# GNN layer and mixture of experts on one core: GpSimd's block loop written out with fixed index columns, two of six gathers moved ahead of the join, the row normalisation on ScalarE moved ahead of the masked copies

## The chip, the cores and the metric

The kernel runs on one core of a Trainium2 chip. The metric is the device time of one execution, in microseconds (us). TensorE (PE in the rows) does the matmuls, VectorE (DVE), ScalarE (ACT) and GpSimd (POOL) the element work, SyncE (SP) only issues transfers. GpSimd also issues every indirect transfer (a gather or a scatter by a column of row numbers).

## The reference

There are 6250 nodes of 256 features and 100000 edges of 96 features, sorted by their target node `dst`. A GNN layer, then a mixture of 16 experts, both with a residual:

```python
xn = layernorm(x)
out1 = segment_sum(edge_attr, dst);  cnt = segment_sum(1, dst)
out2 = where(cnt > 0, segment_max(edge_attr, dst), 0)
out3 = out1 / max(cnt, 1)
h = concat([xn, out1, out2, out3, u[0]])
x = x + (relu(h @ W1 + b1) @ W2 + b2 + xn)
y = layernorm(x);  two best experts of y @ gate_w + gate_b, softmax of the two
moe = weighted sum of the two expert MLPs (256 -> 512 -> 256)
x = x + layernorm(y + moe) * gamma + beta
```

## The kernel before

**Stages.** From 0 to about 117 us indices are made, from there to about 765 us the GNN layer runs, then 113 expert tiles until about 1210 us, then the last sums and norms. The prediction is about the GNN layer.

**Edges.** The edges are cut into ten chunks of 128 pieces of 80 edges. VectorE scans one chunk after another (`edges`), running sums and running maxima from the end of the edge list to its start, and SyncE stores the results to DRAM (`run_sum`, `run_max`, `piece_carry`), raises `chunk_done` when a chunk has landed and then loads the edges of a later one.

**Nodes.** The 6250 nodes are worked off in 25 blocks (`MACROS`) of two tiles (index `a`) of 125 rows, highest nodes first. For block i+1, while TensorE works on block i:

- GpSimd gathers, per tile, the rows of `run_max` (into `GM`), `run_sum` (`GS`) and `piece_carry` (`GC`) at which the nodes begin: six indirect transfers (lines 639 to 641), issued two blocks ahead. The row numbers stand in `IX`, two columns a tile. `gatei` holds, per block, how many chunks must be in DRAM (its level, 1 to 10); GpSimd loads it into a register (line 629), and one of ten branches (line 636) holds the six gathers with that many chunks as the transfers' source.
- `cut` (GpSimd, 646) and `carry_in` (ScalarE, 874 to 882) work out what a node takes from the next piece; `join` (GpSimd, 650 to 654) adds it up into `RAW`; `mask_rows` (ScalarE) makes six masked copies into `NB` (906 to 908), and then the two normalised tiles `XN` (912).
- TensorE's `turn` (1155, 1158) transposes `XN` and `NB`; it waits for `node_rows`, raised by the last operation of `mask_rows`.

**TensorE's step** for block i is: first half of layer 1 (1174, 1176, 1178), router of block i-2 (1207), second half of layer 1, `turn` of block i+1, layer 2 (1188) with `turn_x2` of block i-1 (1200) in its middle. The second half of layer 1 waits for the first half's relu, which ScalarE does (926) behind `carry_in` of block i+1.

**GpSimd's step** (`rows_step`) for block i is: `add_rows` (668; waits until ScalarE has taken layer 2 of block i-1 out, 976), `residual` (685, 687), `cut`, `norm1` (659 to 663) and `join` of block i+1, `norm2` (673 to 678) of block i-1, `gather` of block i+2. Steps 2 to 21 are in a hardware loop of two steps a turn (`in_pairs`); since the block number is then in a register, `gather` first copies the four index columns to `IXn` (631), and waits for that copy.

All engines run in the order in which their code is written, and wait on semaphores alone.

Of the kernel before, what the change touches and what calls it, by code (L numbers as in the profile page):

```python
# [98 lines left out]
def after(i, g, b, n=1):  # L99

    return i + n, g + (b + n) // 2, (b + n) % 2


def gnn_moe_kernel(nc, x, dst, edge_attr, u, gW1, gb1, gW2, gb2, gate_w, gate_b,
# [47 lines left out]
    ALONE = (SURE - 7) // 4 * 4  # L152
    KEYS = 8192
# [40 lines left out]
    with ExitStack() as ctx:  # L194
# [75 lines left out]
        IXn = [a.take(2, 2, parts=NT, dt=U32) for _ in range(2)]  # L270
# [117 lines left out]
        ix_copied, carried, joined, node_rows = sem("ix_copied"), sem("carried"), sem("joined"), sem("node_rows")  # L388
# [191 lines left out]
        def _(pool):  # L580
# [47 lines left out]
            def gather(i, g, b):  # L628
                level = pool.value_load(gatei[0:1, bass.ds(MACROS - 1 - i, 1)], min_val=1, max_val=LEVELS)
                hold(pool, turned, i + 1)  # L630
                pool.tensor_copy(IXn[b], IX[:, bass.ds(2 * (MACROS - 1 - i), 2), :]).then_inc(ix_copied, 1)
                pool.wait_ge(ix_copied, i + 1)
                hold(pool, chunk_done, level * LEVEL)
                for lv in range(1, LEVELS + 1):
                    edges, pieces = lv * LEVEL * P * T, lv * LEVEL * P
                    with pool.If(level == lv):
                        for a in range(2):
                            last, before = (bass.IndirectOffsetOnAxis(IXn[b][:, a, n:n + 1], 0) for n in range(2))
                            pool.indirect_dma_start(out=GM[b][:, a, :], out_offset=None, in_=s_max[0:edges], in_offset=last).then_inc(gathered[b], 16)  # L639
                            pool.indirect_dma_start(out=GS[b][:, a, :], out_offset=None, in_=s_sum[0:edges], in_offset=last).then_inc(gathered[b], 16)  # L640
                            pool.indirect_dma_start(out=GC[b][:, a, :], out_offset=None, in_=carry[0:pieces], in_offset=before).then_inc(gathered[b], 16)
# [47 lines left out]
            def rows_step(i, g, b):  # L689
                more = not isinstance(i, int) or i + 1 < MACROS  # L690
                norm = not isinstance(i, int) or i >= 1
                if norm:
                    add_rows(i - 1)
                residual(i, g, b)
                if more:
                    cut(*after(i, g, b))
                    norm1(i + 1)
                    join(*after(i, g, b))
                if norm:
                    norm2(i - 1)  # L700
                if not isinstance(i, int) or i + 2 < MACROS:
                    gather(*after(i, g, b, 2))
            pool.sem_inc(joined, 1)
            gather(0, 0, 0)
# [3 lines left out]
            gather(1, 0, 1)  # L708
            rows_step(0, 0, 0)
            rows_step(1, 0, 1)  # L710
            pool.wait_ge(index_ready, 2)
            in_pairs(pool, MACROS, rows_step, ahead=3, first=2)
# [96 lines left out]
        def _(act):  # L809
# [91 lines left out]

            def mask_rows(i, g, b):
                act.wait_ge(joined, i + 2)
                for a in range(2):
# [3 lines left out]
                    act.activation(NB[b][:, a, 2 * P:3 * P].rearrange("p (n r) -> p n r", n=QUAD), spread(RAW[b][:, a, 0, EF - REST:EF], 1, QUAD),  # L908
                                   ACT.Identity, scale=rch[:, j])
                act.wait_ge(rstd1_ready, i + 1)  # L910
                for a in range(2):
                    ins = act.activation(XN[b][:, a, :], XR[b][0:NT, a, :], ACT.Identity, bias=nmr_1[:, a:a + 1], scale=rstd_1[:, a:a + 1])  # L912
# [66 lines left out]
            def gnn_step(i, g, b, to=None):  # L979
# [19 lines left out]
                if more:  # L999
                    mask_rows(*after(i, g, b))  # L1000
# [859 lines left out]
```

## Time and profile before

| | us |
|---|---|
| median of 3 runs (1270.43 to 1273.61) | 1272.97 |
| the profiled execution | 1271.26 |
| its span, first to last instruction | 1269.4 |
| PE busy | 1097.0 (86%) |
| POOL busy | 807.2 (64%) |
| DVE busy | 832.5 (66%) |
| ACT busy | 647.6 (51%) |

The page and the views of the trace count time in us from the span's start. "busy" leaves out what an engine's queue does for itself (register work, branches, waits, the issuing of plain transfers); such records stand under POOLq, ACTq or SPq. A bracket at a row's end says how long the engine stood idle ahead of that row, and what ended it.

### The profile page before, as it was taken

The numbers are of one execution on the slowest core, as the hardware profiler recorded it, in microseconds if no ns is written. First come the engines' busy times: TensorE is split into PE (matmuls) and PEld (weight loads), VectorE is DVE, ScalarE is ACT, GpSimd is POOL, SyncE is SP. The second block draws the span as 40 slices with busy tenths as digits, with TensorE's granted clock in tenths as the row PEclk, the third lists the DMA queues.
The fourth block names the chain that finished last, engine by engine and source line by source line (L and its number), as shares of the span: only waits on it lengthen the run. The fifth ranks groups of instructions, "written<-read, shape, count | busy, mean of one in ns | idle before, by whom it ended". The sixth has DMA issues, their size and how long they took to land.

```text
span 1269.4 us, 27454 instructions
## 1 busy us (share of the span) xinstructions
PE 1097.0 (86%) x6460; PEld 955.6 (75%) x6461; DVE 832.5 (66%) x3164; ACT 647.6 (51%) x1974; POOL 807.2 (64%) x1056
## 2 busy tenths in 40 slices
PE   2002999999999999999999999889999999999935
PEld 1002888888888888887888788789999999999911
DVE  4989999899989989980367811366322222247788
ACT  5863565566556656665566534222323232345554
POOL 4886657666666666666676525556666566657586
PEclk7555999999999999998999999899999999999975
DMA  9995768777776785479111146776666676688855
GB/s 318 282 306 181 256 232 311 253 271 286 268 259 249 293 259 204 169 286 315 54 38 47 30 154 203 261 250 200 204 209 213 205 217 214 208 295 293 282 178 155
DMA packets 131327, 282.70 MB, mean 223 GB/s; under 512 B 25900, under 2 KB 38576, under 8 KB 131114
## 3 DMA queue, kind: packets, MB, share of 16 engines
q1 hardware_dynamic: 94230, 218.41, 50.2%
q0 software_dynamic: 26048, 43.47, 11.3%
q10 hardware_dynamic: 10964, 19.96, 4.6%
q14 instruction: 64, 0.52, 0.1%
q8 instruction: 21, 0.34, 0.1%
HBM read 167.27 MB, written 114.25 MB: 222 GB/s over the span
## 4 chain that ended last, share of the span: by engine, by line
PE 57%; POOL 11%; issue 10%; DMA 8%; ACT 7%; DVE 3%; POOLq 2%; ACTq 1%; SPq 0%; DVEq 0%
PE ps L1299 16%; PE ps L1307 15%; PE ps L1188 7%; PE ps L1174 7%; PE ps L1176 6%; DMA mem<-piece_carry,mem 4%; DMA mem<-in_dst_dram,mem 2%; POOL mem L639 2%; POOL mem L640 2%; POOL mem L622 2%; PE ps L1285 2%; ACT mem L926 1%; POOL mem L791 1%; PE ps L1178 1%; POOL mem L797 1%
## 5 line engine op out<-in xcount | busy, mean ns | idle before, releaser
L1026 ACT ACTIVATE mem<-ps,mem 128x128 f32<-128x128 f32 x452 | 129.3, 368 | 284.6 <-PE ps L1299 283.8
L1299 PEld LDWEIGHTS ps<-mem 128*128 128x128 f32 x1808 | 220.6, 194 | 18.9 <-issue 12.2
L1299 PE MATMUL ps<-mem 128*128 128x128 f32 x1808 | 224.8, 278 | 10.2 <-issue 9.6
L1174 PE MATMUL ps<-mem 128*128 128x250 f32 x800 | 209.3, 384 | 11.7 <-ACT mem L926 10.0
L1307 PE MATMUL ps<-mem 128*128 x904 | 214.8, 381 | 0.7 <-issue 0.7
L1396 DVE TENSOR_TENSOR_SCAN mem<-ps,mem 128x80 f32<-128x80 f32 x960 | 208.0, 304 | 0.3
L1400 DVE TENSOR_TENSOR_SCAN mem<-ps,mem 128x80 f32<-128x80 f32 x960 | 207.9, 308 | 0.0
L1176 PE MATMUL ps<-mem 128*128 128x250 f32 x800 | 205.0, 379 | 0.0
L1188 PE MATMUL ps<-mem 128*125 128x256 f32 x800 | 182.4, 381 | 0.7 <-ACT mem L926 0.7
L1307 PEld LDWEIGHTS ps<-mem 128*128 128x128 f32 x904 | 163.8, 191 | 18.8 <-issue 0.9
L1174 PEld LDWEIGHTS ps<-mem 128*128 128x128 f32 x800 | 153.3, 194 | 31.6 <-ACT mem L926 12.3
L1176 PEld LDWEIGHTS ps<-mem 128*128 128x128 f32 x800 | 154.1, 193 | 18.8
L1188 PEld LDWEIGHTS ps<-mem 128*125 128x125 f32 x800 | 147.3, 189 | 21.5 <-ACT mem L926 1.1
L1679 DVE TENSOR_TENSOR mem<-ps,mem 128x256 f32<-128x256 f32 x113 | 48.0, 425 | 150.9 <-PE ps L1307 115.6
L734 POOL DMA_INDIRECT expert_rows<-mem x90 | 91.6, 1018 | 85.6 <-DVE mem L1679 66.1
L1672 DVE COPY mem<-ps 128x256 f32<-128x256 f32 x113 | 47.8, 423 | 136.4 <-PE ps L1285 132.8
L727 POOL DMA_INDIRECT mem<-x_normed,mem x96 | 96.1, 1001 | 34.0 <-issue 16.8
L926 ACT ACTIVATE mem<-ps,mem 128x250 f32<-128x250 f32 x200 | 77.1, 468 | 46.5 <-PE ps L1178 46.5
L1155 PE MATMUL ps<-mem 125*128 125x125 f32 x100 | 20.6, 288 | 90.8 <-ACT mem L912 90.8
L639 POOL DMA_INDIRECT mem<-run_max,mem x50 | 63.8, 1277 | 46.4 <-issue 46.1
L1155 PEld LDWEIGHTS ps<-mem 125*128 125x128 f32 x100 | 11.5, 144 | 97.9 <-issue 97.9
L622 POOL DMA_INDIRECT mem<-in_dst_dram,mem x50 | 62.8, 1255 | 27.2 <-issue 12.5
(284 smaller groups left out, 1677.2 us busy)
## 6 DMA issues: line engine op xcount, KB each, us to landing
mem<-in_L_ffn_w_dram SPq DMA_DIRECT2D x129, 512.0 KB, 9.4
run_sum<-mem SPq DMA_DIRECT2D x80, 480.0 KB
run_max<-mem SPq DMA_DIRECT2D x80, 480.0 KB
mem<-in_edge_attr_dram SPq DMA_DIRECT2D x72, 480.0 KB, 8.2
mem<-expert_rows SPq DMA_DIRECT2D x26, 256.0 KB, 5.5
x_rows<-mem ACTq DMA_DIRECT2D x25, 256.0 KB, 4.4
x_normed<-mem ACTq DMA_DIRECT2D x25, 256.0 KB
mem<-in_x_dram ACTq DMA_DIRECT2D x24, 256.0 KB
```

The lines of the kernel that those rows point to most:

```text
L639: pool.indirect_dma_start(out=GM[b][:, a, :], out_offset=None, in_=s_max[0:edges], in_offset=last).then_inc(gathered[b], 16)
L727: pool.indirect_dma_start(out=XG[q], out_offset=None, in_=x2_d[0:rows], in_offset=bass.IndirectOffsetOnAxis(slot_now[q % 2], 0)).then_inc( ...
L734: pool.indirect_dma_start(out=ya_d, out_offset=bass.IndirectOffsetOnAxis(into_now[b], 0), in_=YO[b], in_offset=None).then_inc(yo_stored[b] ...
L926: act.activation(H[:, hc, :], bank(H_BANKS[q][hc - q * QUAD], 0, M), ACT.Relu, bias=cbias[:, hc:hc + 1]).then_inc(h_ready, 1)
L1026: ins = act.activation(hT[b][:, c, :], bank(2 + b, c * P, (c + 1) * P), ACT.Relu, bias=eb1c[:, bass.ds(e, 1), c])
L1174: pe.matmul(h, W1x[:, c, hc * P:(hc + 1) * P], XT[b][:, c, :], start=(c == 0), stop=False)
L1176: pe.matmul(h, W1a[:, s, hc * P:(hc + 1) * P], AT[b][:, s, :], start=False, stop=False)
L1188: ins = pe.matmul(bank(5, a * D, (a + 1) * D, NT), H[:, hc, a * NT:(a + 1) * NT], W2[:, hc, :], start=(hc == 0), stop=(hc == HC - 1))
L1299: ins = pe.matmul(bank(2 + b, f * P, (f + 1) * P), w1now[q][:, c, f * P:(f + 1) * P], XgT[b][:, c, :], start=(c == 0), stop=(c == DC - 1))
L1307: ins = pe.matmul(bank(6 + b, 0, D), hT[b][:, c, :], w(c * D, D), start=(c == 0), stop=(c == FC - 1))
L1396: ins = dve.tensor_tensor_scan(out=Sb[:, ::-1, f], data0=keep[b][:, ::-1], data1=Eb[b][:, ::-1, f], initial=0.0, op0=ALU.mult, op1=ALU.add)
L1400: ins = dve.tensor_tensor_scan(out=Eb[b][:, ::-1, f], data0=bound[b][:, ::-1], data1=Eb[b][:, ::-1, f], initial=-FMAX, op0=ALU.min, op1=AL ...
```

## The change

- GpSimd's step is written out 25 times with the block number as a constant. The six gathers read their columns of `IX` in place; the copy to `IXn`, the wait for it and the wait for `turned` are gone.
- The ten branches become at most two. `SCANNED` holds, per block, a number of chunks `near`; a block of a level up to `near` waits for `near` chunks and gathers from them, one of a higher level waits for all ten. Where `near` is ten there is no branch and no load. For the input of the reference the levels of blocks 0 to 24 are 1, 1, 1, 1, 2, 2, 2, 2, 2, 3, 3, 3, 3, 4, 4, 4, 5, 5, 5, 6, 6, 7, 7, 8, 10, and `near` is 1, 1, 1, 1, 2, 2, 3, 3, 3, 4, 4, 5, 5, 6, 6, 7, 7, 8, 8, 9, 9, 9, 10, 10, 10, so that the second branch is never taken.
- Of the six gathers of block i+2 the first `AMID` = 2 (`GM` and `GS` of tile 0) are issued behind `norm1` and ahead of `join` of block i+1, the other four behind `norm2` of block i-1. They were all six behind `norm2`.
- On ScalarE the two `XN` operations stand ahead of the six masked copies, as `norm_rows`.

```diff
+    SCANNED = [1 if i < 4 else min(LEVELS, 1 + (24 * (i - 2) + 10) // 52) for i in range(MACROS)]
+    AMID = 2
...
-            def gather(i, g, b):
-                level = pool.value_load(gatei[0:1, bass.ds(MACROS - 1 - i, 1)], min_val=1, max_val=LEVELS)
-                hold(pool, turned, i + 1)
-                pool.tensor_copy(IXn[b], IX[:, bass.ds(2 * (MACROS - 1 - i), 2), :]).then_inc(ix_copied, 1)
-                pool.wait_ge(ix_copied, i + 1)
-                hold(pool, chunk_done, level * LEVEL)
-                for lv in range(1, LEVELS + 1):
-                    edges, pieces = lv * LEVEL * P * T, lv * LEVEL * P
-                    with pool.If(level == lv):
...
+            def by_level(i, body):
+                near = SCANNED[i]
+                if near == LEVELS:
+                    body(LEVELS)
+                else:
+                    level = pool.value_load(gatei[0:1, MACROS - 1 - i:MACROS - i], min_val=1, max_val=LEVELS)
+                    with pool.If(level < near + 1):
+                        body(near)
+                    with pool.If(level > near):
+                        body(LEVELS)
...
+                def behind_cut(levels):
+                    if levels:
+                        pool.wait_ge(chunk_done, levels * LEVEL)
+                        gather_rows(i + 2, 0, AMID, levels)
+                    if i + 1 < MACROS:
+                        join(*after(i, g, b))
+                    if i:
+                        norm2(i - 1)
+                    if levels:
+                        gather_rows(i + 2, AMID, 6, levels)
...
+            for i in range(MACROS):
+                rows_step(i)
...
+            def norm_rows(i, g, b):
+                act.wait_ge(rstd1_ready, i + 1)
+                for a in range(2):
+                    act.activation(XN[b][:, a, :], XR[b][0:NT, a, :], ACT.Identity, bias=nmr_1[:, a:a + 1], scale=rstd_1[:, a:a + 1])
...
                 if more:
+                    norm_rows(*after(i, g, b))
                     mask_rows(*after(i, g, b))
```

GpSimd's queue in one step of the block loop, before, from `join` on (`mem` is the core's SBUF; ISA and branch rows are the queue's own work):

```order
L650 TENSOR_TENSOR mem<-mem 125x2x96 [waits carried]
L651 TENSOR_TENSOR mem<-mem 125x192
L652 TENSOR_TENSOR mem<-mem 125x192
L654 TENSOR_TENSOR mem<-mem 125x2x96 [waits picked]
L673 TENSOR_SCALAR mem<-mem 125x2 [waits moments2_step]
L676 TENSOR_TENSOR mem<-mem 125x2 [waits norm2_step]
L678 TENSOR_TENSOR mem<-mem 125x2 [waits norm2_step]
L629 TENSOR_LOAD mem
L629 ISA x2
L631 COPY mem<-mem 125x4 [waits turned]
L636 COMPARE_AND_BRANCH [waits ix_copied,chunk_in_dram]
L639 DMA mem<-run_max,mem 125x96
```

The same place now, from the last operation of `norm1` (L676 in the new numbering) on:

```order
L644 TENSOR_LOAD mem
L644 ISA x2
L645 COMPARE_AND_BRANCH
L636 DMA mem<-run_max,mem 125x96 [waits chunk_in_dram]
L636 DMA mem<-run_sum,mem 125x96
L663 TENSOR_TENSOR mem<-mem 125x2x96 [waits carried]
L664 TENSOR_TENSOR mem<-mem 125x192
L665 TENSOR_TENSOR mem<-mem 125x192
L667 TENSOR_TENSOR mem<-mem 125x2x96 [waits picked]
L686 TENSOR_SCALAR mem<-mem 125x2 [waits moments2_step]
L689 TENSOR_TENSOR mem<-mem 125x2 [waits norm2_step]
L691 TENSOR_TENSOR mem<-mem 125x2 [waits norm2_step]
```

The load of the level, the branch and two gathers now stand ahead of the join (L663 to L667), and four gathers follow the last row; the copy is gone.

ScalarE's queue ahead of the first `turn`, before, behind the last operation of `carry_in`:

```order
L906 ACTIVATE mem<-mem 125x192 [waits joined]
L907 ACTIVATE mem<-mem 125x64
L908 ACTIVATE mem<-mem 125x128
L906 ACTIVATE mem<-mem 125x192
L907 ACTIVATE mem<-mem 125x64
L908 ACTIVATE mem<-mem 125x128
L912 ACTIVATE mem<-mem 125x256 [waits norm1_rstd_ready]
L912 ACTIVATE mem<-mem 125x256
```

And now:

```order
L929 ACTIVATE mem<-mem 125x256 [waits norm1_rstd_ready]
L929 ACTIVATE mem<-mem 125x256
L935 ACTIVATE mem<-mem 125x192 [waits joined]
L936 ACTIVATE mem<-mem 125x64
L937 ACTIVATE mem<-mem 125x128
L935 ACTIVATE mem<-mem 125x192
L936 ACTIVATE mem<-mem 125x64
L937 ACTIVATE mem<-mem 125x128
```

The two 125x256 operations now stand ahead of the wait for `joined`, and the masked copies are the last thing ahead of `node_rows`.

## Rows read from the trace of the kernel before

**Rows 1.** Waits of PE, 95 to 765 us: total us, times, longest us
```profile
PE ps L1155 <- ACT mem L912: 90.8, 1, 90.8
PE ps L1174 <- ACT mem L926: 10.0, 13, 2.5
```
**Rows 2.** Timeline of PE, block starts and one `turn`: start us, us, operation
```profile
172.19 1.01 PE L1174 MATMUL ps<-mem 128*128 128x250 f32 x4
...
375.62 1.01 PE L1174 MATMUL ps<-mem 128*128 128x250 f32 x4
...
391.58 0.43 PE L1155 MATMUL ps<-mem 125*128 125x125 f32 x2
...
400.04 1.01 PE L1174 MATMUL ps<-mem 128*128 128x250 f32 x4
...
628.39 1.01 PE L1174 MATMUL ps<-mem 128*128 128x250 f32 x4
```
**Rows 3.** Timeline of PE in block 7
```profile
306.30 1.11 PE L1174 MATMUL ps<-mem 128*128 128x250 f32 x4 [1.36 <-ACT mem L926]
307.25 1.62 PE L1176 MATMUL ps<-mem 128*128 128x250 f32 x4
```
**Rows 4.** Timeline of POOL in block 10 and the start of block 11
```profile
382.63 0.20 POOL L663 TENSOR_TENSOR mem<-mem 125x2 f32<-125x2 f32 x1
383.59 0.59 POOL L650 TENSOR_TENSOR mem<-mem 125x192 f32<-125x192 f32 x1 [0.76 <-ACT mem L882]
...
385.38 0.60 POOL L654 TENSOR_TENSOR mem<-mem 125x192 f32<-125x192 f32 x1
...
388.99 0.20 POOL L678 TENSOR_TENSOR mem<-mem 125x2 f32 x1 [0.27 <-POOL mem L676]
...
391.65 1.33 POOL L639 DMA_INDIRECT mem<-run_max,mem  x1 [1.43 <-issue]
393.28 1.21 POOL L640 DMA_INDIRECT mem<-run_sum,mem  x1 [0.30 <-issue]
...
399.35 1.21 POOL L641 DMA_INDIRECT mem<-piece_carry,mem  x1 [0.30 <-issue]
401.18 1.43 POOL L668 TENSOR_TENSOR mem<-mem 125x512 f32<-125x512 f32 x1 [0.62 <-ACT mem L976]
```
**Rows 5.** Chain that ended last, block 2, then block 10: start us, us, what
```profile
186.01 1.24 POOLq L629
...
389.13 0.29 POOLq L629
...
390.73 0.92 issue
...
399.35 6.83 DMA mem<-piece_carry,mem
```
**Rows 6.** Waits of POOL, 100 to 765 us: the gaps ahead of the copy
```profile
POOL mem L631 <- issue: 25.1, 24, 2.0
```
**Rows 7.** Timeline of ACT in block 10: first masked copy, the two normalisations
```profile
388.16 0.45 ACT L906 ACTIVATE mem<-mem 125x192 f32<-125x192 f32 x1 [0.92 <-ACT mem L940]
...
389.93 1.08 ACT L912 ACTIVATE mem<-mem 125x256 f32<-125x256 f32 x2
```
**Rows 8.** Timeline of POOL, ACT and PE at the start of the layer
```profile
95.28 0.20 POOL L631 COPY mem<-mem 125x4 uint32<-125x4 uint32 x1
96.52 1.22 POOL L639 DMA_INDIRECT mem<-run_max,mem  x1 [1.04 <-issue]
...
116.35 1.08 ACT L912 ACTIVATE mem<-mem 125x256 f32<-125x256 f32 x2
...
117.69 0.65 PE L1155 MATMUL ps<-mem 125*128 125x125 f32 x2 [90.75 <-ACT mem L912]
```
**Rows 9.** Timeline of SP: edge loads, issued when the third chunk is done
```profile
198.04 4.42 SPq L440 DMA_DIRECT2D mem<-in_edge_attr_dram  x8
```
**Rows 10.** Timeline of PE in block 22: the expert tables' matmul
```profile
706.85 0.76 PE L1224 MATMUL ps<-mem 125*128 125x172 bf16 x4 [2.30 <-DVEq L1522]
```

More of the change, by code:

```diff
@@ new lines, in gather_rows @@
+            def gather_rows(i, lo, hi, levels):
+                b = i % 2
+                edges, pieces = levels * LEVEL * P * T, levels * LEVEL * P
+                for n in range(lo, hi):
+                    j, a = 2 * (MACROS - 1 - i) + n // 3, n // 3
+                    into, rows = ((GM[b], s_max[0:edges]), (GS[b], s_sum[0:edges]), (GC[b], carry[0:pieces]))[n % 3]
+                    kind = 1 if n % 3 == 2 else 0
+                    pool.indirect_dma_start(out=into[:, a, :], out_offset=None, in_=rows,
+                                            in_offset=bass.IndirectOffsetOnAxis(IX[:, j, kind:kind + 1], 0)).then_inc(gathered[b], 16)
@@ new lines, in by_level, with gather, all_rows @@
+            def by_level(i, body):
[8 more added lines that the diff above has]
+                        body(LEVELS)
+            def gather(i):
+                def all_rows(levels):
+                    pool.wait_ge(chunk_done, levels * LEVEL)
+                    gather_rows(i, 0, 6, levels)
+                by_level(i, all_rows)
@@ L687, in residual, with rows_step @@
                 pool.tensor_tensor(RES, RES, b2bc, ALU.add).then_inc(residual_ready, 1)
[L689 to L692, printed above, removed]
+            def rows_step(i):
+                g, b = i // 2, i % 2
+                def behind_cut(levels):
+                    if levels:
+                        pool.wait_ge(chunk_done, levels * LEVEL)
+                        gather_rows(i + 2, 0, AMID, levels)
[5 more added lines that the diff above has]
+                        gather_rows(i + 2, AMID, 6, levels)
+                if i:
                     add_rows(i - 1)
                 residual(i, g, b)
-                if more:
+                if i + 1 < MACROS:
                     cut(*after(i, g, b))
                     norm1(i + 1)
[L698 to L702, printed above, removed]
+                if i + 2 == (TILES - LATE) // 2:
+                    pool.wait_ge(index_ready, 2)
+                if i + 2 < MACROS:
+                    by_level(i + 2, behind_cut)
+                else:
+                    behind_cut(0)
             pool.sem_inc(joined, 1)
-            gather(0, 0, 0)
+            gather(0)
             norm1(0)
@@ L707, in _ @@
             join(0, 0, 0)
[L708 to L712, printed above, removed]
+            gather(1)
+            for i in range(MACROS):
+                rows_step(i)
             def next_from(i, h, q):
@@ L907, in mask_rows @@
                     act.activation(NB[b][:, a, 2 * EF:2 * P], RAW[b][:, a, 0, 0:EF - REST], ACT.Identity, scale=rch[:, j])
[L908 to L912, printed above, removed]
+                    ins = act.activation(NB[b][:, a, 2 * P:3 * P].rearrange("p (n r) -> p n r", n=QUAD), spread(RAW[b][:, a, 0, EF - REST:EF], 1, QUAD),
+                                         ACT.Identity, scale=rch[:, j])
                 ins.then_inc(node_rows, 1)
```

9 lines of the change are left out of this document (2 added, 7 removed).

## The prediction

> **What bounds the kernel now.** I read the page's table of slices first: PE is at eight tenths or more from the fifth slice on to the last two, so any gain must come from the start, from PE's few waits, or from the last stage, which the change doesn't touch. The waits of PE in the GNN stage [rows 1] are two things: 90.8 us until the first `turn`, ended by the last normalisation on ACT, and 13 waits of 10.0 us in all for the first relu. The block starts [rows 2] give the size of the second: blocks 2 to 19, 18 of them, take 628.39 - 172.19 = 456.20 us. Block 10 takes 400.04 - 375.62 = 24.42 with PE never idle, and 18 of these are 439.56. So 16.6 us are lost, more than the 10.0 of waits, because a long wait is followed by slow matmuls: behind 1.36 us idle in block 7 four matmuls take 1.62 us and not 1.01 [rows 3].
>
> The relu is late because ACT stands in `carry_in`, waiting for the last gather. In block 10 that gather is issued at 399.35 and lands 6.83 us later, at 406.18, which is 6.14 into block 11 [rows 4, 5]; there it costs 0.48 us, and block 11 is one of the mild ones. POOL can't issue it sooner: its six gathers begin 2.66 us behind the start of the last `norm2` operation (391.65 - 388.99) and are 1.5 us apart [rows 4]. **So POOL's chain of one step sets the loss, at the landing of the sixth gather.**
>
> **The start (-1.9 us).** Ahead of the first gather the copy goes: it starts at 95.28 and the gather at 96.52, 1.24 us later; a gap of 0.30 as between two gathers is left, which saves 0.94 [rows 8, 4]. `norm1` of block 0 is long done when ACT reaches the masked copies (ACT then waits for the join), so the two normalisations, 116.35 to 117.43, leave the path: 1.0 us saved. Together 1.9, all on the path, as PE waits for nothing else there.
>
> **POOL's step.** In block 10 `norm1`'s last operation starts at 382.63. Behind it now come the load, the branch and two gathers. The load of the level ended 0.43 behind the start of the operation ahead of it (389.13 + 0.29 against 388.99); between the last branch and the first gather lie 0.92 us [rows 4, 5]. Register work between load and branch isn't separable from the copy's in these rows; it lies between 0.1 and 1.3 us (the branch at 390.73 follows the load's end by 1.31 with the copy in between), and I take 0.4, nearer the low end, since the copy, its semaphore and one or two branches go. So the first gather starts 0.43 + 0.4 + 0.92 = 1.75 us behind, at 384.38, the second 1.63 later at 386.01, and the join at 387.25. The join lasts 2.39 (383.59 to 385.98), to 389.64. It ended at 385.98 before: **3.7 us later**, of which the 0.76 wait for `carry_in` in front of it was free anyway.
>
> Who waits for that is ACT, with the masked copies, then relu and the taking out of `turn`, queued behind. ACT reaches them at 388.16 [rows 7]; now it first does the normalisations there, to about 389.2, and then waits for the join. From 389.70 the six copies last 1.85 (388.16 to 389.93, and a tail of 0.1), and PE sees them 0.26 later (117.69 against 117.43 [rows 8]), at 391.81. PE gets to `turn` at 391.58 [rows 2]. **So each block may wait about 0.25 us at `turn`, a wait that wasn't there.** Without the edit on ACT it would be 1.1 more. The bounds: with the first gather starting as soon as a gather follows another (0.30 for 0.92) there is none; with the whole 2.66 us of rows 4 kept, 0.9 more, 1.15.
>
> Some loads of the level are long: 1.24 us at 186.01 against 0.29 at 389.13 [rows 5]. The gaps ahead of the copy sum to 25.1 us in 24 [rows 6]; at 0.87, a quick one's length, they would be 20.9, so the long loads cost 4.2, or 0.18 a step. They were absorbed in POOL's step; now they stand ahead of the join and reach PE: 18 x 0.18 = 3.3 us.
>
> The Trainium skill, Runtime: NRT & Kernel Launch, Instruction fetch mechanics, has a register load at about 200 ns each, a round trip. The quick loads of this trace are near it (0.29), the long ones aren't; by the page's figure, an estimate, these 3.3 us would be nought. The trace decides, and I keep them.
>
> What it buys: `norm2` now follows the join, and its three operations end at about 391.4, and four gathers follow, the last starting at about 396.9 instead of 399.35, 2.5 us earlier. With the same 6.83 it lands at 403.7, 3.7 into block 11, ahead of `cut` (405.3) and `carry_in`. POOL is free at about 398.1, 2.9 us ahead of `add_rows` (401.18), where it had 0.6 [rows 4]. So the waits at the relu should go, all 16.6 us, slow matmuls with them.
>
> **Free edits.** Waiting for `near` chunks and not for the level: the tightest case is the third chunk, done at 198.04 [rows 9] and first asked for in block 4 at about 229; nothing waits. The branches to 2 from 10, the `turned` wait and the loop's own branches go without a price; they lay in the gap of 2.66 or beside gathers.
>
> **Blocks 20 to 24.** PE waits there for VectorE's tables (2.30 us at 706.85 [rows 10]), which start from the router's logits of an earlier block; they move with the earlier blocks, and nothing further is gained or lost.
>
> **The sum**, against the profiled execution's 1271.26 (span 1269.4): start -1.9; blocks 0 and 1 at 0.25 each, +0.5; blocks 2 to 19: 18 x (24.42 + 0.25) + 3.3 = 447.4 for 456.2, -8.8. Together -10.2, or 1261.1. The median of the runs is 1.7 above the profiled one; against it the forecast is 1272.97 - 10.2 = **1262.8 us**.
>
> **Rivals.** (B) The join is never late: the 0.92 us in front of the first gather runs while `norm1` does, and long loads hide in the same place. For it: between two gathers only 0.30 is seen. Against: the gap was there at 390.73 with nothing else to do. It gives the start and all of 16.6: 1272.97 - 18.5 = 1254.5.
>
> (C) **Slower: the join is late and takes the place of the relu.** Its place is `turn`; its price the upper bound, 1.15 + 0.18 = 1.33 us in each of 20 blocks, 26.6, against 18.5 gained: 1281. Waits of that length were followed by slow matmuls [rows 3], which would add to it. It decides from a mean lateness of 18.5 / 20 = 0.93 us. Against it: my 0.25 would have to be out by 0.7, and POOL's step starts no later than in block 10, since `add_rows` now has slack.
>
> (D) The landing doesn't follow the issue: the four last gathers meet the stores of the scanned chunks, and land as late as ever, or the small waits at `turn` and at a few relus add up to what the relu's did. Then the start alone is left: about 1271. Against: 2.5 us earlier is a third of the 6.83.
>
> (E) The unrolled code stalls at its branches. The rows have ten branches a step, and a jump back every second step, without a gap of a transfer's length in them. If each skipped body cost a wait like one landing (6.83) less the 2.9 of slack, 20 x 3.9 less 18.5 would give 1332. The Trainium skill, same page and section, says that a taken branch whose target isn't in the current window makes the queue fetch it by DMA before going on; it also says that this favours full unrolling. By that rule this rival's place is behind the sixth gather, where two branches are taken.
>
> **How the numbers follow.** Forecast 0.52 (alone 1258 to 1268, the 0.25 and the 0.18 being free within about 0.3 a block), B 0.20, C 0.10, D 0.16, E 0.02. A measurement of this kernel tells about 0.3%, 3.8 us, from no change. Faster by more holds the forecast, B and a sliver (0.02) of D, 0.74; the same is the rest of D, 0.14; slower C and E, 0.12. The range 1254 to 1272 leaves out C, E, a part of D and the low end of B.
>
> **What would show it.** The first `turn` at about 115.8 us instead of 117.69. PE's waits for ACT's relu near nought, and in their place waits at `turn`, some 20 of about 0.25 and three to five of 1 us, behind long loads. On POOL 1.75 us from `norm1`'s last operation to the first gather. No row of POOL waiting for SP's chunks. Block starts 24.5 to 24.8 apart. The prediction is wrong if blocks 2 to 19 take under 442 or over 452 us, or if the part behind block 19 changes by more than 2.

## The result and the profile after

The changed kernel takes 1253.32 us (median of 4 runs, 1251.29 to 1254.82), where the kernel before takes 1272.97. The ratio is 0.985, with a 95% interval of 0.982 to 0.987: 19.6 us less, nearly twice the 10.2 that I forecast, and 0.7 us outside my range. The profiled execution is 1254.82 us long, with a span of 1252.9, against 1271.26 and 1269.4 before. So the two traces, on which all that follows rests, explain 16.4 us; the other 3.2 are how each profiled execution stands to its own median (1.7 below it before, 1.5 above it after). In the later runs a few executions are more than 1.5% longer than the fastest of their kernel, and the ratios leave those out.

First the waits of PE, 95 to 765 us, of the kernel after (total us, times, longest us), which answer to [rows 1]. `turn` is now line 1183, layer 1 is 1202, the masked copies end on 937 and the relu is 952.

```profile
PE ps L1183 <- ACT mem L937: 89.7, 7, 87.7
...
PE ps L1202 <- ACT mem L952: 1.7, 3, 0.7
```

The waits for the relu were 10.0 us in 13 and are 1.7 in 3. The waits at `turn` are 7, one of which is the first block's 87.7, so 2.0 us are left for the other six. Now PE's timeline, with the first `turn` of the layer, the starts of blocks 0, 2, 10, 11 and 20, the longest of the six waits and the `turn` of block 10; it answers to [rows 2, 8].

```profile
115.64 0.65 PE L1183 MATMUL ps<-mem 125*128 125x125 f32 x2 [87.73 <-ACT mem L937]
...
119.38 1.20 PE L1202 MATMUL ps<-mem 128*128 128x250 f32 x2 [1.43 <-ACT mem L945]
...
170.11 1.01 PE L1202 MATMUL ps<-mem 128*128 128x250 f32 x4
...
366.68 1.01 PE L1202 MATMUL ps<-mem 128*128 128x250 f32 x4
...
382.64 0.43 PE L1183 MATMUL ps<-mem 125*128 125x125 f32 x2
...
391.10 1.01 PE L1202 MATMUL ps<-mem 128*128 128x250 f32 x4
...
603.70 0.43 PE L1183 MATMUL ps<-mem 125*128 125x125 f32 x2 [0.52 <-ACT mem L937]
...
612.17 1.01 PE L1202 MATMUL ps<-mem 128*128 128x250 f32 x4
```

The first `turn` came at 117.69 and comes at 115.64: 2.05 us at the start, in this pair of executions (more on that at e1). Blocks 2 to 19 take 612.17 - 170.11 = 442.06 us and took 456.20: 14.14. Blocks 0 and 1 take what they took (50.73 for 50.76), and so do blocks 20 to 23; 0.3 us less lie behind them. That is the whole 16.4, within a tenth. The floor of 18 x 24.42 = 439.56 is nearly reached, and block 10, at 391.10 - 366.68 = 24.42, has no wait at `turn`.

POOL in block 10, which answers to [rows 4]:

```profile
373.44 0.19 POOL L676 TENSOR_TENSOR mem<-mem 125x2 f32<-125x2 f32 x1
374.87 1.32 POOL L636 DMA_INDIRECT mem<-run_max,mem  x1 [1.24 <-issue]
376.50 1.21 POOL L636 DMA_INDIRECT mem<-run_sum,mem  x1 [0.31 <-issue]
377.74 0.60 POOL L663 TENSOR_TENSOR mem<-mem 125x192 f32<-125x192 f32 x1
...
379.52 0.60 POOL L667 TENSOR_TENSOR mem<-mem 125x192 f32<-125x192 f32 x1
...
386.94 1.21 POOL L636 DMA_INDIRECT mem<-piece_carry,mem  x1 [0.30 <-issue]
392.14 1.28 POOL L681 TENSOR_TENSOR mem<-mem 125x512 f32<-125x512 f32 x1 [3.99 <-ACT mem L1002]
```

The sixth gather starts 20.3 us into the block, and started at 23.7; `add_rows` (line 681) finds POOL idle for 3.99 us where it was 0.62. The join, 377.74 to 380.12, ends 13.4 us into the block, where it ended at 10.4. From here on a time "into the block" counts from the first layer-1 matmul of that block.

What stands between `norm1`'s last operation and the first gather is to be seen in the chain that ended last, a step with a short load (block 10) and one with a long load (block 16): start us, us, what.

```profile
373.40 0.23 POOLq L644
373.63 0.10 issue
373.73 0.16 POOLq L644
...
373.97 0.04 POOLq L645
374.01 0.86 issue
374.87 1.32 POOL mem L636
...
520.21 0.23 POOLq L644
520.44 0.81 issue
521.25 0.15 POOLq L644
...
521.47 0.04 POOLq L645
521.51 0.86 issue
```

The load of the level (line 644) shows in the chain as 0.23 us and then as an "issue" of 0.10 us in one case and 0.81 in the other, which is the rest of the same load: it lasts 0.3 us in the first case and 1.0 in the second. The branch (645) costs 0.04 and is followed by 0.86 us in both. These are the two parts of my 1.75 us, and I come back to them.

### The profile page after: what moved, and what is told of

It is laid out like the page before. It is cut to its first block, busy times and chain, and to the rows that moved or that the text cites. A ratio compares the mean times of both kernels' runs of the same rounds, so it can differ in the third digit from the quotient of the medians.

```text
span 1252.9 us, 26862 instructions
## 1 busy us (share of the span) xinstructions
PE 1088.9 (87%) x6460; PEld 949.9 (76%) x6461; DVE 838.2 (67%) x3164; ACT 650.1 (52%) x1974; POOL 804.0 (64%) x1030
## 4 chain that ended last, share of the span: by engine, by line
PE 40%; POOL 29%; issue 17%; DVE 4%; ACT 4%; DMA 4%; POOLq 1%; SPq 0%; DVEq 0%; ACTq 0%
PE ps L1327 16%; PE ps L1335 15%; POOL mem L636 12%; DMA mem<-in_dst_dram,mem 2%; POOL mem L698 2%; POOL mem L681 2%; POOL mem L700 2%; PE ps L1216 2%; PE ps L1313 2%; PE ps L1202 2%; PE ps L1204 2%; ACT mem L852 2%; POOL mem L623 1%; POOL mem L689 1%; POOL mem L674 1%
## 5 line engine op out<-in xcount | busy, mean ns | idle before, releaser
L1327 PE MATMUL ps<-mem 128*128 128x128 f32 x1808 | 223.8, 278 | 10.9 <-issue 10.4
L1202 PE MATMUL ps<-mem 128*128 128x250 f32 x800 | 205.4, 379 | 3.1 <-ACT mem L952 1.7
L1204 PE MATMUL ps<-mem 128*128 128x250 f32 x800 | 202.2, 375 | 0.0
L681 POOL TENSOR_TENSOR mem<-mem 125x512 f32<-125x512 f32 x25 | 32.6, 1303 | 118.2 <-ACT mem L1002 118.2
```

The costliest lines, as they stand in the source:

```text
L1202: pe.matmul(h, W1x[:, c, hc * P:(hc + 1) * P], XT[b][:, c, :], start=(c == 0), stop=False)
L1204: pe.matmul(h, W1a[:, s, hc * P:(hc + 1) * P], AT[b][:, s, :], start=False, stop=False)
L1327: ins = pe.matmul(bank(2 + b, f * P, (f + 1) * P), w1now[q][:, c, f * P:(f + 1) * P], XgT[b][:, c, :], start=(c == 0), stop=(c == DC - 1))
```

## The experiments

All are compared with the kernel before on their own chip, whose median was 1275.22 us for the first four, 1272.06 for the next four and 1278.06 for the last four. Three stretches that hardly depend on the edits differ by some us from execution to execution: what lies ahead of block 2 (it starts at 170.1 to 173.5 us, in e8 at 177.2), block 22 (29.8 to 33.3 us long) and what lies behind the start of block 24, the expert stage above all (527 to 536 us). The kernel after alone has 170.1 and 173.2 for the first and 31.7 and 33.3 for the second in its two profiled executions. So the totals scatter, and the sharper number of each trace is the length of blocks 2 to 19, the stretch in which the change acts. All of it in one table (the last two columns are the lowest and the highest of blocks 2 to 18, in us into the block, from POOL's timeline). The first column is the median of all executions; the ratio is worked out from the single executions and differs from that of the two medians by up to 0.003:

```
                                         us  ratio [95%]             blocks 2-19                join ends   6th gather
before                              1272.97                       628.39-172.19=456.20  10.3-13.0   23.7-26.9
after                               1253.32  0.985 [0.982,0.987]  612.17-170.11=442.06  13.4-14.5   20.2-21.5
e1_after_again                      1256.96  0.983 [0.979,0.988]  615.20-173.22=441.98  13.3-14.5   20.2-21.3
e2_norms_behind                     1272.4   0.997 [0.996,0.999]  628.33-173.12=455.21  13.4-14.4   20.2-21.2
e3_none_ahead                       1251.82  0.980 [0.976,0.984]  609.83-170.39=439.44  10.2-10.7   21.5-21.7
e4_one_ahead                        1251.92  0.980 [0.976,0.985]  611.47-172.02=439.45  11.8-12.8   20.2-21.2
e5_norms_only                       1281.74  (see there)          632.53-170.82=461.71  10.2-14.2   23.7-28.6
e6_none_ahead_norms_behind          1248.63  0.981 [0.977,0.985]  609.73-170.28=439.45  10.2-10.7   21.5-21.6
e7_load_early                       1252.13  0.983 [0.979,0.987]  610.55-171.11=439.44  12.8-13.2   19.6-20.0
e8_three_ahead                      1288.13  1.011 [1.007,1.015]  646.53-177.19=469.34  14.9-15.9   20.2-21.8
e9_unrolled_only                    1269.5   0.995 [0.992,0.997]  624.35-173.49=450.86  10.1-12.5   22.8-26.6
e10_ten_branches                    1257.08  0.984 [0.982,0.986]  611.49-170.94=440.55  10.1-10.9   22.4-23.9
e11_copy_back                       1259.34  0.985 [0.982,0.988]  611.11-171.73=439.38  10.2-10.7   21.5-21.9
e12_two_copies                      1256.0   0.982 [0.979,0.985]  612.89-173.51=439.38  10.2-10.7   21.6-22.0
```

**The change once more.** The kernel after without an edit.

> The changed kernel as it is, timed again beside the kernel before and the three variants of this series. The two profiled executions differ by 16.4 us and the medians by 19.6. If the profiled execution of the changed kernel was a long one of its own spread, the new ratio lies at 0.985 to 0.987 and blocks 2 to 19 again take about 442 us; if the difference of the medians is real beyond the trace, a part outside blocks 2 to 19 must be shorter in this trace.

It was 1256.96 us, a ratio of 0.983, with 442.0 us for blocks 2 to 19: the gain and its place are both there again. The start isn't. The first `turn` comes 1.53 us later than in the first execution of the same kernel, and block 2 starts at 173.22, 1.0 us later than in the kernel before:

```profile
117.17 0.65 PE L1183 MATMUL ps<-mem 125*128 125x125 f32 x2 [88.53 <-ACT mem L937]
```

**ScalarE's edit undone.** The kernel after, with

```
-    norm_rows(*after(i, g, b))
     mask_rows(*after(i, g, b))
+    norm_rows(*after(i, g, b))
```

> ScalarE's edit undone: the two normalisations behind the masked copies again, all else as changed. Theory (the join now ends at 13.4 us of a block and turn is due at 15.96): copies and normalisations need 2.85 us behind the join and 0.26 to reach TensorE, so turn waits 0.65 us in a plain block and 0.6 more behind a long load: 20 x 0.65 + 4, and 1.0 at the start, about 16 us more than the changed kernel, 1269. Rival (the edit is worth only its 1.0 us at the start): 1254.5.

It was 1272.4 us, 15.4 more than e1 where I expected about 16, and the join's end stayed where the kernel after has it. PE in block 10 of this kernel, and ScalarE ahead of that (the masked copies are lines 936 to 938 here, the normalisations 929):

```profile
391.52 0.43 PE L1183 MATMUL ps<-mem 125*128 125x125 f32 x2 [1.08 <-ACT mem L929]
```
```profile
388.62 0.46 ACT L936 ACTIVATE mem<-mem 125x192 f32<-125x192 f32 x1 [2.66 <-POOL mem L667]
...
390.09 0.39 ACT L938 ACTIVATE mem<-mem 125x128 f32<-125x128 f32 x1
390.38 1.08 ACT L929 ACTIVATE mem<-mem 125x256 f32<-125x256 f32 x2
```

ScalarE had stood idle for 2.66 us until the join was done, copied, and then normalised, and PE waited 1.08 us for it at `turn`. So in the kernel after ScalarE's edit carries nearly the whole gain (13.2 us in blocks 2 to 19). The next runs say that the edit by itself isn't worth 13 us.

**No gather ahead of the join, and one.** The kernel after with

```
-    AMID = 2
+    AMID = 0
```

and, for the other, `AMID = 1`.

> AMID = 0: all six gathers behind norm2, with fixed columns and two branches. Theory (the gain is the dropped copy, its wait and the branches, since the sixth gather then starts at 22.5 us of a block and lands at 4.9 of the next, just ahead of cut at 5.0): 1253 to 1257, with waits at the relu of 0 to 3 us in all and none at turn. Rival (the two gathers ahead of the join are what frees the chain): most of the old waits stay, 1262 to 1270.

> AMID = 1: one gather ahead of the join. Theory: the join ends at 11.9 us of a block instead of 13.4, norm2 still ends at 13.5 because it waits for ScalarE, and the sixth gather starts at 20.4 as against 20.2; so the 2.0 us of waits at turn go and nothing is lost: 1251 to 1252. Rival (each gather ahead of the join buys 1.5 us of landing that some blocks need): up to 1256.

Neither was slower than the kernel after; in the stretch both are 2.6 us shorter, with no wait at `turn` behind the first block's. PE's waits of e3, 95 to 765 us, and then POOL in its block 10, whose start is at 365.69:

```profile
PE ps L1183 <- ACT mem L937: 87.6, 1, 87.6
```
```profile
375.43 0.60 POOL L667 TENSOR_TENSOR mem<-mem 125x192 f32<-125x192 f32 x1
377.45 0.19 POOL L686 TENSOR_SCALAR mem<-mem 125x2 f32<-125x2 f32 x1 [1.42 <-ACT mem L966]
...
378.69 0.20 POOL L691 TENSOR_TENSOR mem<-mem 125x2 f32<-125x2 f32 x1 [0.18 <-POOL mem L689]
379.50 1.33 POOL L636 DMA_INDIRECT mem<-run_max,mem  x1 [0.61 <-issue]
...
387.21 1.21 POOL L636 DMA_INDIRECT mem<-piece_carry,mem  x1 [0.31 <-issue]
```

All six gathers come behind `norm2`, and still the sixth starts 21.5 us into the block and not 23.7. From the start of `norm2`'s last operation to the first gather it is 0.81 us, where [rows 4] had 2.66. So the rival of e3, that the two early gathers free the chain, is out. The two gathers that the change put ahead of the join buy only the last 1.2 us, and nothing waits for these.

**ScalarE's edit alone, on the kernel before.** The normalisations go ahead of the masked copies, and nothing on POOL changes:

```
-                act.wait_ge(rstd1_ready, i + 1)
-                for a in range(2):
-                    ins = act.activation(XN[b][:, a, :], ...
...
+                norm_rows(*after(i, g, b))
                 mask_rows(*after(i, g, b))
```

> The kernel before with ScalarE's edit alone (normalisations in front of the masked copies); GpSimd's loop, copy, level branches and gathers as they were. Theory (ScalarE's edit is worth something only at the start and where GpSimd's join is late; in the kernel before the join ends at T+10.4 and the normalisations end ahead of the turn at T+15.96): only the 1.0 us at the start, 1272 where before is 1273, ratio 0.999, blocks 2 to 19 still near 456 us. Rival (the normalisations on the way to the turn cost every block by themselves): about 0.8 us in each of 20 blocks, 1257, ratio 0.987.

It gained nothing: blocks 2 to 19 took 461.7 us in the profiled execution of 1273.12 us. Its four executions took 1270.85, 1273.12, 1290.37 and 1293.12 us, too far apart for a ratio; the two short ones lie on either side of 1272.06, the median of the kernel before. The waits for the relu (line 928 here) were 15.4 us in 10, as they were 10.0 in [rows 1]:

```profile
PE ps L1178 <- ACT mem L928: 15.4, 10, 3.7
```

The rival (12 us or more gained) is out. The theory's 456 was 5.7 too low; what the late gathers cost varies more than I had allowed for, with three blocks of 30.3 to 30.4 us in this execution.

**No gather ahead and ScalarE's edit undone.** Both edits, of e2 and of e3, on the kernel after; what is left of the change is on POOL: the loop written out, fixed columns without the copy, and one load and two branches, which still stand ahead of the join.

> The kernel after with no gather ahead of the join and with ScalarE's edit undone: only GpSimd's unrolled loop with fixed index columns remains. Theory: the join ends at T+10.3 and the order on ScalarE no longer matters, blocks 2 to 19 stay at 439.5 us, no wait at the turn; 1.0 us more than with both (the start), so a ratio of 0.981 to the kernel before. Rival (ScalarE's edit carries about 16 us whatever GpSimd does, as undoing it in the kernel after seemed to say): 455 us for blocks 2 to 19, ratio 0.994 or above.

This is the decisive run: 439.45 us in blocks 2 to 19, within a hundredth of e3's, and one wait at `turn`, the first block's.

```profile
PE ps L1183 <- ACT mem L929: 89.5, 1, 89.5
...
PE ps L1202 <- ACT mem L952: 1.7, 3, 0.7
```

So what ScalarE's edit carried in e2 was the damage of the two early gathers. They end the join 3.1 us later; slack takes up most of that, and the edit takes 1.0 us off the way from the join's end to the last operation ahead of `turn` (3.0 us in e2, 2.0 in the kernel after), which is enough. Take both away and the gain is whole, with 1248.63 us the lowest median of the study. Whether it beats the kernel after as a whole isn't shown: the two ratios' intervals overlap (0.977 to 0.985, and 0.979 to 0.988 in e1), and only the stretch, 2.6 us shorter, tells them apart. Nor is the 1.0 us that I gave ScalarE's edit at the start seen in it: the first gather starts at 95.80 us here and at 95.83 in e3, the first `turn` at 116.86 and 115.92, but block 1 at 146.01 and 146.12.

**The level's load ahead of `add_rows`.** The kernel after with

```
+                level = load_level(i + 2)
                 if i:
                     add_rows(i - 1)
...
-                    level = pool.value_load(gatei[0:1, MACROS - 1 - i:MACROS - i], min_val=1, max_val=LEVELS)
```

> The kernel after with the level's load moved to the front of GpSimd's step, ahead of add_rows, where GpSimd waits for TensorE's output anyway. Theory (the few waits at the turn in the kernel after come from loads of the level that take 0.9 us in place of 0.3, between norm1 and the first gather): first gather about 1.1 us behind norm1 in place of 1.43, no wait at the turn in blocks 2 to 19, these take 439.6 to 440 us in place of 442.1, total 2 us below the kernel after (ratio about 0.983). Rival (the waits at the turn come from something else): the distance stays 1.43 and 442 stays.

The stretch fell to 439.44 us, the few waits at `turn` are gone, and the first gather starts 0.88 us behind `norm1`'s last operation (681 here), with the branch alone between them:

```profile
373.17 0.20 POOL L681 TENSOR_TENSOR mem<-mem 125x2 f32<-125x2 f32 x1
374.05 1.32 POOL L636 DMA_INDIRECT mem<-run_max,mem  x1 [0.68 <-issue]
```

With the load out of the way the join never ends later than 13.2 us into blocks 2 to 18, so a long load reaches nobody. Both numbers are better than I expected (1.1 us, and 439.6 to 440). The 2.6 us don't show in the total.

**Three gathers ahead.** `AMID = 3`.

> The kernel after with three gathers ahead of the join in place of two. Theory (join's end moves by 1.52 us a gather and the kernel after has about 0.25 us of room left): join ends at T+14.95, the turn comes about 1.2 us late in each of blocks 2 to 19, 442 becomes 461 to 465 us, total about 1278, ratio near 1.003. Rival (gathers issued earlier land earlier and give back what the join loses): no more than 1258.

It is slower than the kernel before, as my rival C had it, and by its mechanism: 22 waits at `turn`, 21 of them sum to 29.7 us. PE's waits of e8, and one `turn`, where POOL's load was a long one:

```profile
PE ps L1183 <- ACT mem L937: 119.2, 22, 89.5
```
```profile
400.08 0.43 PE L1183 MATMUL ps<-mem 125*128 125x125 f32 x2 [1.58 <-ACT mem L937]
```

469.34 us are 6 us over the middle of what I expected of the stretch, 461 to 465, at 1.2 us a block. The join ended at 14.9 to 15.9 us into the block, not always at 14.95; nine of the eighteen blocks are 26.0 us or longer. One more gather ahead costs (469.34 - 442.06) / 18 = 1.5 us a block, and the kernel after stands less than half a us from that step.

**Only unrolled.** The kernel before with

```
-            in_pairs(pool, MACROS, rows_step, ahead=3, first=2)
+            for i in range(2, MACROS):
+                rows_step(i, i // 2, i % 2)
```

> The kernel before with GpSimd's block loop written out (blocks 2 to 24) and nothing else: the copy of the index columns, the level's register, its ten branches and ScalarE's order stay. In the kernel before GpSimd takes 2.46 us from norm2's last operation to the first gather and ends its sixth at T+23.7 to T+25.9; with no gather ahead and fixed columns it is 0.61 us and T+21.5. Theory (what counts is how late the last gather is issued, and most of the 2.2 us are the copy, its wait and the branches): norm2 0.3 us shorter, the gathers 0.3 to 0.6 us earlier, blocks 2 to 19 take 450 to 455 us, total about 1269. Rival (the dynamic index in the loop is what costs): gathers 1.5 us or more earlier, blocks 2 to 19 at 443 or below, total 1259 or below.

450.86 us, 5.3 less than in the kernel before. That stretch varies by as much between the kernel before and e5, which have the same POOL; but the total's ratio of 0.995, from eight runs, says that something is gained. The middle one of the sixth gathers starts at 24.0 us into the block here and at 24.8 in the kernel before; long loads of the level, of 1.4 us, eat a part of what the loop's registers gave back. The copy (631) waits 1.66 us for one in block 10:

```profile
382.63 0.20 POOL L678 TENSOR_TENSOR mem<-mem 125x2 f32<-125x2 f32 x1 [0.18 <-POOL mem L676]
384.48 0.19 POOL L631 COPY mem<-mem 125x4 uint32<-125x4 uint32 x1 [1.66 <-issue]
386.04 1.33 POOL L639 DMA_INDIRECT mem<-run_max,mem  x1 [1.37 <-issue]
```

**Ten branches again.** The kernel after with no gather ahead, and with load and branches behind `norm2`:

```
-                    with pool.If(level < near + 1):
-                        body(near)
-                    with pool.If(level > near):
-                        body(LEVELS)
+                for lv in range(1, LEVELS + 1):
+                    with pool.If(level == lv):
+                        body(lv)
```

> The kernel after with no gather ahead of the join, and with the level's load and ten branches behind norm2 as in the kernel before, but on fixed columns and without the copy. Theory (branches and the load cost GpSimd 0.3 us, 0.15 us a branch not taken and about 0.9 us from branch to gather): first gather at T+14.9 in the first blocks and T+16 in the last of 2 to 19, last gather T+22.6 to T+23.7, so landings late only in the later of these blocks; blocks 2 to 19 take 441 to 447 us. Rival (the branches cost nothing, the copy was all): below 440 us, as with no gather ahead.

440.55 us, 1.1 more than e3, and a little less than expected: the sixth gather starts at 22.4 to 23.9 us, and six of the eighteen cuts come a little late. So with all else in place the load's and the branches' place and number are worth 1.1 us of the stretch. From `norm2`'s last operation to the first gather it is 1.75 us here:

```profile
380.11 0.20 POOL L686 TENSOR_TENSOR mem<-mem 125x2 f32<-125x2 f32 x1 [0.18 <-POOL mem L684]
381.86 1.33 POOL L636 DMA_INDIRECT mem<-run_max,mem  x1 [1.56 <-issue]
```

**The copy back, once and twice.** No gather ahead, and ahead of the six

```
+                    pool.tensor_copy(IXn[b], IX[:, j:j + 2, :]).then_inc(ix_copied, 1)
+                    pool.wait_ge(ix_copied, i + 1)
```

> The kernel after with no gather ahead of the join, and with the copy of the index columns and the wait for it put back ahead of the six gathers. Theory: the first gather 0.6 to 0.9 us later (T+14.4 to T+14.7), the last at about T+22.3, which is 2.1 us ahead of the next block; its rows still land ahead of the cut at T+5.0 and blocks 2 to 19 stay at 439.5 to 440 us, total as with no gather ahead (ratio 0.981). Rival (the landing was late because of the copy itself, whose wait lets other transfers in): 445 us or more.

> As the run with the copy put back, with the copy and its wait twice: a plain delay of GpSimd by another 0.3 to 0.5 us. Theory: last gather at about T+22.7, first late landings, blocks 2 to 19 take 440 to 443 us; the two runs together say from which issue time the landing is late. Rival (landing does not follow issue): the same as with one copy, however late the issue.

Both leave the stretch at 439.38 us. I had expected 0.6 to 0.9 us from one copy; it costs 0.05, since most of it lies in the gap that stands in front of the first gather anyway (0.53 us here, and 0.61 in e3):

```profile
380.00 0.20 POOL L697 TENSOR_TENSOR mem<-mem 125x2 f32<-125x2 f32 x1 [0.18 <-POOL mem L695]
380.14 0.19 POOL L636 COPY mem<-mem 125x4 uint32<-125x4 uint32 x1
380.86 1.33 POOL L642 DMA_INDIRECT mem<-run_max,mem  x1 [0.53 <-POOL mem L636]
```

The second copy moved the sixth gather by 0.02 to 0.45 us, and one cut came late by 0.5 us; that is too little to tell anything on the slope, and my 440 to 443 was missed. e11's 1259.34 us, 7.5 more than e3's (beside a kernel before that was 2.8 us longer, too), isn't the copy: up to block 24 its trace is 3.0 us longer, in block 22 (31.5 for 29.9) and the start, and the rest of the 6.2 us lies in the expert stage.

**When a landing is late.** The fourteen traces (before, after and the twelve runs) hold 252 blocks of 2 to 19. I set the start of the sixth gather against the start of the block that uses it, and call a cut late that starts more than 5.3 us into that block (it is at 5.0 where nothing holds it up):

```
sixth gather starts                     blocks   late cuts   latest cut, us into the block
over 2.0 us ahead of the block             185           1       5.5
0 to 2.0 us ahead of it                     50          24       7.9
behind the block's start                    17          16       9.6
```

What the cut waits for is seen in e5, where the trace has the landing of nine of these gathers: seven of the nine cuts are late, and six of the seven start 0.15 to 0.17 us behind that landing, which came 6.1 to 8.9 us behind the gather's start. The kernel before issues between 3.0 ahead and 0.8 behind, with 14 late cuts in 18; the kernel after between 4.2 and 3.5 ahead, with none.

## Why the prediction was wrong

**What held.** The bound: POOL's chain sets the landing of the sixth gather, which makes the relu late. e3, e6, e9 and e10 all follow it, in the order of their sixth gathers. The free edits and blocks 20 to 23 came out at nought. No row of POOL waits for SP's chunks. Slow matmuls vanished with the waits: the 10.0 us of waits were 16.6 of time, and e3 gives back all of it.

**The start** is not shown. 2.05 us for 1.9 was a hit in this pair alone, as e1 has 0.52. I gave 0.94 us of it to the copy ahead of the first gather; that gather starts at 96.52 us in the kernel before and at 95.87 after, but at 96.56 in e1, and at 95.87 in e5, which still has the copy. The 1.0 us of ScalarE's edit is there at the first `turn` and gone by block 1 (e3 and e6).

**The step that failed is the wait of 0.25 us at `turn`**, 5 us in 20 blocks, and under it the 1.75 us from `norm1`'s last operation to the first gather. The gap is 374.87 - 373.44 = 1.43. The load ends 0.26 behind that operation's start and not 0.43 (in the kernel before the computing of its address stands in the queue ahead of it); from there to the branch it is 0.27 and not 0.4; behind the branch it is 0.90, as I had 0.92. Another 0.25 us came from the other side: `norm1` itself ends earlier in the block (6.76 us into it for 7.01), because `cut` no longer waits for a landing. I had put all of the join's new time on top of a block that was itself still late. Together the join ends at 13.44 and not at 14.02 us into the block. And the hand-over to PE was too long in my sum: I took 0.26 us from the start of the layer, but where `turn` waits in the block loop it starts 0.05 us behind ScalarE's last copy (0.05 to 0.06 in every block of the kernel after and of e8 in which it waits). In block 10 of the kernel after that copy ends at 382.13, 15.45 us into the block:

```profile
381.74 0.39 ACT L937 ACTIVATE mem<-mem 125x128 f32<-125x128 f32 x1
```

`turn` could start at 15.50 and starts at 15.96, when PE gets to it. So what was to be 0.25 us too late is 0.46 too early. A term that small, next to a limit, and worked out from a gap that I guessed at 0.4, should have been a coin's throw between the forecast and rival B. B's 1254.5 is 1.2 us from the measured median, by luck; its reason, that the 0.92 us run beside `norm1`, is wrong: they are there, and e7 has them too, 0.88 with the branch alone. In block 20, where the level needs neither load nor branch, a row of POOL has no such gap:

```profile
618.78 0.20 POOL L676 TENSOR_TENSOR mem<-mem 125x2 f32<-125x2 f32 x1
619.17 1.32 POOL L636 DMA_INDIRECT mem<-run_max,mem  x1 [0.19 <-issue]
```

**The long loads** were 3.3 us in the sum. They do occur, seven of them in steps 2 to 18, 0.9 to 1.0 us long for 0.3; but slack takes off the first part of each, and those of blocks 6 and 18 don't arrive at all. Five of the six waits at `turn`, 1.5 us of the 2.0, are theirs. The sixth, 0.52 us in block 19, is something that I hadn't seen: three of POOL's operations there take 1.11, 0.99 and 1.26 us for 0.60, 0.60 and 0.72, and the join ends at 14.6 us into the block. This isn't chance: e1 has the same three within 0.01 us. In both traces they run beside operations of VectorE on the router's logits (lines 1517 to 1523), of which it has none in blocks 2 to 18; but two more of POOL's run beside the first of these (598.48 and 599.03) and take their usual 0.6. Whether VectorE is the cause wasn't tested.

```profile
599.58 1.11 POOL L665 TENSOR_TENSOR mem<-mem 125x192 f32<-125x192 f32 x1
```
```profile
600.28 1.03 DVE L1518 TENSOR_TENSOR mem<-mem 125x576 f32<-125x576 f32 x1
```
With the slow matmuls behind them, all six waits cost 442.06 - 439.56 = 2.5 us. The Trainium skill (Runtime: NRT & Kernel Launch, Instruction fetch mechanics) has such a load at some 200 ns a register; most are near that with 0.29, the long loads are at 0.9 to 1.0 here and at 1.4 in e9. The sum by that figure, without the 3.3 us, would have been nearer the result, for a wrong reason; e7, which takes all loads out of this path, the long and the quick, shows the 2.6 us gone, those of block 19 with them.

**The sum.** Start -2.05 for -1.9; blocks 0 and 1 -0.03 for +0.5; blocks 2 to 19 -14.1 for -8.8; what lies behind, -0.3 for 0. Of the 6.2 us by which the profiled pair beats my sum, 5 are the wait at `turn`, 0.8 what I gave to long loads and they didn't cost, even with block 19's counted to them (3.3 for 2.5), and the rest the start and the end. **The other miss is the standing to the median:** I took the profiled execution's 1.7 us for a fixed offset, while the profiled execution of the kernel after was the longest of its four, which made 3.2 us. Without that the median would have been 1256.5, inside the range; e1, beside the kernel before on another chip, has 18.3 us between the medians.

**What the change's parts are worth** was right in sign only. I took the two early gathers for the part that brings the landing forward, by 2.5 us. Of the 3.5 us by which the sixth gather of block 10 is earlier they bring 1.2 (e3 against the kernel after), which nobody waits for, and they cost the 2.6 us that e3 and e6 have over the kernel after in the stretch. The 2.2 us that count come from the code in front of the gathers, that is from the load and the branches taken from behind `norm2` to a place ahead of the join, where POOL waits for `carry_in` anyway, and from registers, loop and copy. The time from the start of `norm2`'s last operation to the first gather, as a mean over blocks 2 to 18, says how much each took: 3.12 us in the kernel before, 2.89 in e9, 2.21 in e10, 0.87 in e11, 0.82 in e3. So the loop is 0.2 of it, the copy with its waits 0.7, the load and the branches 1.4, the most. In the stretch it looks different, 5.3, 10.3 and 1.1 us, since those depend on what has been taken away already: in e10 the sixth gathers still start late, but from block 3 on 0.6 to 2.0 us ahead of the block that uses them, and only six cuts are late; what is taken away beyond that gains little. How the 10.3 us between e9 and e10 divide wasn't tried part by part. Long loads are a share of them, as the two block 10's show, and the copy, with its own wait, costs nothing where the load and the branches no longer stand in front of it (e11). ScalarE's edit, which e10 has and e9 hasn't, gained nothing by itself (e5).

Rival C was real, with a place one gather further on (e8). D is out: the landing follows the issue, by the table of 252 blocks. E is out, too: no gap that POOL has ahead of a gather of the layer in its unrolled code, other than by waiting for another engine, is over 2.3 us in the kernel after, far from a landing's length. The Trainium skill (Runtime: NRT & Kernel Launch, Instruction fetch mechanics) says that a taken branch to a target outside the window has to fetch, and that kernels prefer unrolling for it; here the ratio of the loop written out and nothing else is 0.995 [0.992, 0.997], which agrees in sign, but the rows show it as shorter register work, not as a fetch.

## What to carry to other kernels

Where an engine's late issue sets a late landing, look first at what stands between the last real operation and the first issue, registers, a small copy, loads of a scalar and branches, and take it away or move it into a wait that the engine has anyway; the two together were worth the whole gain here (e6). Moving the issues themselves ahead of someone else's input (the join) makes two edits depend on each other: undoing the second then seems to show that it is worth 13 us, when the two undone together cost nothing. An edit's worth is only known from the kernel without its partner, and a wait of 0.25 us worked out from rows is a bet on both signs: here it came out as 0.46 us of room.

## What the runs showed of the hardware

- From the end of a branch on POOL's queue to the next indirect DMA it is 0.86 to 0.92 us (after, e7, [rows 5]). Behind a small operation with no branch between it is 0.61 (`norm2`'s last, e3) or 0.19 (`norm1`'s last, block 20 of the kernel after), and behind another gather 0.30. The price of the branch is the same if it is the only thing there (e7).
- A load of one scalar on POOL's queue takes 0.3 us in most of the steps 2 to 18 of the kernel after and 0.9 to 1.0 us in seven; 1.4 us were seen in e9. I haven't found what the long loads coincide with.
- In block 19 of the kernel after, three of POOL's operations took 1.6 to 1.9 times as long as in block 10, beside VectorE's operations on the router's logits, and in e1 again. The cause wasn't tested.
- A copy of 4 columns with a wait for its own semaphore, ahead of an indirect DMA, cost 0.05 us.
- A sixth gather that starts more than 2.0 us ahead of the block is in time in 184 of 185 blocks, one that starts within 2.0 us in 26 of 50.
- The start of block 2 (170.1 and 173.2 us in two executions of the kernel after), block 22 (29.8 to 33.3 us) and the expert stage (527 to 536) vary between executions, the last two without any edit that touches them, and set how far a total can be read.
